# A depthwise convolution shared between VectorE and TensorE: 128 and 64 channels in place of 96 and 96, two taps a product, two products side by side, the image loop written out

## The reference, cut to the phase

```python
D, inner = 96, 192                    # k_conv has shape (3, 3, 1, inner): depthwise
DECAY, GAIN = 0.6, 0.4                # of _ema_scan: y[i] = DECAY * y[i-1] + GAIN * x[i]
h  = _layernorm(x, n1_g, n1_b)
p  = h @ w_in + b_in                  # 96 -> 192 channels
p  = depthwise 3x3 convolution of p with k_conv, zero padding
p  = p + 0.25 * (scans of p along both axes, forward and backward)
p  = _layernorm(p, on_g, on_b)
x  = x + p @ w_out + b_out            # 192 -> 96 channels
```

## Time and profile before

| | us |
|---|---|
| median of 3 runs | 1366.96 |
| lowest, highest | 1360.24, 1372.87 |
| the profiled execution | 1367.83 |
| its span in the profile | 1366.0 |
| TensorE, VectorE busy in the span | 1183.3 (87%), 741.9 (54%) |
| ScalarE, POOL busy | 510.8 (37%), 391.8 (29%) |

### The profile page before, as it was taken

How to read it: one execution, slowest core, us unless ns; L and a number is a source line. 1 busy time by engine, 2 the same in 40 slices (tenths; PEclk the granted TensorE clock), 3 DMA queues, 4 the chain that set the end, 5 groups by cost and what they waited for, 6 DMA issues and landing times. The chain is left out here.

```text
span 1366.0 us, 24417 instructions
## 1 busy us (share of the span) xinstructions
PE 1183.3 (87%) x8951; PEld 812.9 (60%) x8951; DVE 741.9 (54%) x2104; ACT 510.8 (37%) x823; POOL 391.8 (29%) x599
## 2 busy tenths in 40 slices
PE   0599989699996979999999997786988978799998
PEld 0266656477775656666667664564454544477776
DVE  1578873367774426666666666474355565232322
ACT  0266643233331333333343331442443422254553
POOL 1356636433433530110110210313200000344432
PEclk9899999899996999999999998788799999799999
DMA  5320000000000000000000000000000000000000
GB/s 67 67 53 2 2 1 1 0 1 0 0 0 1 0 0 1 1 1 1 1 1 1 1 1 1 1 1 1 1 2 1 2 1 1 1 7 13 6 12 12
DMA packets 27297, 9.16 MB, mean 7 GB/s; under 512 B 25345, under 2 KB 27200, under 8 KB 27200
## 3 DMA queue, kind: packets, MB, share of 16 engines
q1 hardware_dynamic: 24720, 7.13, 2.8%
q10 hardware_dynamic: 2480, 0.73, 0.4%
HBM read 6.27 MB, written 1.57 MB: 6 GB/s over the span
## 5 line engine op out<-in xcount | busy, mean ns | idle before, releaser
L142 POOL TENSOR_TENSOR ln_v<-MV,eps 128x2 f32<-128x2 f32 (+3 forms) x81 | 16.1, 199 | 433.6 <-PE bank L1064 246.0
L1126 ACT ACTIVATE fa_e<-bank 128x1024 f32<-128x1024 f32 x64 | 65.5, 1024 | 159.5 <-PE bank L1034 159.5
L1876 PEld LDWEIGHTS bank<-e_w,ex_G 128*128 128x128 f32 x768 | 90.7, 192 | 14.8 <-issue 14.6
L1981 DVE SCALAR_TENSOR_TENSOR X<-bank,ex_L,X 128x96 f32<-128x96 f32 (+1 forms) x128 | 31.7, 310 | 121.1 <-PE bank L1876 113.0
L1178 DVE TENSOR_REDUCE fa_z<-bank 128x4 f32<-128x1024 f32 x64 | 78.3, 1223 | 25.1 <-PE bank L1016 23.3
L1868 PE MATMUL bank<-hT,e_w 96*128 96x512 f32 x192 | 91.0, 610 | 0.0
L1876 PE MATMUL bank<-e_w,ex_G 128*128 128x96 f32 x768 | 90.0, 274 | 0.0
L1918 ACT ACTIVATE ex_G<-bank,e_b 128x512 f32<-128x512 f32 x96 | 64.7, 687 | 63.3 <-PE bank L1868 61.4
L1735 DVE TENSOR_REDUCE ca_z<-bank 128x2 f32<-128x256 f32 x96 | 48.8, 550 | 69.3 <-PE bank L1492 69.2
L1034 PE MATMUL bank<-fa_a,fa_b 64*128 64x256 f32 x512 | 73.5, 406 | 1.1 <-DVE fa_a L1185 1.1
L145 POOL TENSOR_TENSOR ln_r<-ln_v,minus_half 128x2 f32<-128x2 f32 (+3 forms) x81 | 71.7, 885 | 0.0
(11 more groups left out here) (251 smaller groups left out, 2604.0 us busy)
## 6 DMA issues: line engine op xcount, KB each, us to landing
X<-in_x SPq DMA_DIRECT2D x16, 96.0 KB
out_tokens<-X SPq DMA_DIRECT2D x8, 192.0 KB, 2.1
e_w<-in_L_ffn_w SPq DMA_DIRECT2D x2, 576.0 KB
bias0r<-in_L_conv_rpb_table ACTq DMA_DIRECT2D x16, 24.0 KB
m0w<-in_L_conv_mlp_w SPq DMA_DIRECT2D x2, 144.0 KB
m1w<-in_L_conv_w SPq DMA_DIRECT2D x2, 144.0 KB
f_w<-in_L_ffn_W SPq DMA_DIRECT2D x2, 142.5 KB
mixer<-in_mixer SPq DMA_DIRECT2D x1, 256.0 KB
```

Source lines behind the costliest of these rows:

```text
L1126: act.activation(E[v % 2][:], k.banks[:, b:b + 2, :].rearrange("p i (c q) -> p i c q", c=2), ACT.Exp).then_inc(s["exp"], 1)
L1876: last = pe.matmul(bank[6 + e % 2][:, t * C:(t + 1) * C], G[e % 2][:, j, t * P:(t + 1) * P], k.ew2[:, e, j, :], start=(j == 0), stop=(j == ...
```

## The change

The two halves of the convolution get unequal shares: 128 channels for VectorE, which works on partitions in parallel, and 64 for TensorE. TensorE's 64 channels lie twice on the 128 partitions, the second copy shifted by one column of the image, so that a product with K = 128 takes two taps (x = 0 and 1) at once. Nine products become six: three with two taps and three with one (x = 2), whose upper 64 rows of `diag` are zero. They are 64 columns wide and go in turn to partitions 0 to 63 and 64 to 127 of bank 3, so that two lie side by side in the array. Those two sums are added and transposed at once in `conv_t`, by a product with `stack2`, two 64x64 identity matrices on top of each other. `mix` comes after the first pair, and writes bank 7 in place of bank 4. `back` and `conv_t` each begin with one `keep_warm` into bank 4, ahead of their waits. `widened` becomes three activations. `pipeline` becomes `in_turn`, which writes all 16 images out. POOL calls `norm(0, 0)` first and makes `diag` with three products and a memset. The loads grow from 7 transfers to 18, all in `k.late`.

```diff
+def in_turn(steps, body):
+    for n in range(steps):
+        body(n, n % 2, n == 0, n == steps - 1)
...
-    k.win = weight("w_in", [C, CI], a["L1_conv_w_in"])
-    k.bin = weight("b_in", [C, 2], a["L1_conv_b_in"].rearrange("(j p) -> p j", p=C))
-    k.kconv = sb("k_conv", [C, 2, 9])
-    for j in range(2):
-        loads.append((k.kconv[:, j, :], a["L1_conv_k_conv"].rearrange("a b o (j p) -> j p (a b o)", p=C)[j]))
-    k.ong = weight("on_g", [C, 2], a["L1_conv_on_g"].rearrange("(j p) -> p j", p=C))
-    k.onb = weight("on_b", [C, 2], a["L1_conv_on_b"].rearrange("(j p) -> p j", p=C))
-    k.wout = weight("w_out", [C, 2, C], a["L1_conv_w_out"].rearrange("(j p) c -> p j c", p=C))
+    k.win = sb("w_in", [C, 2 * P])
+    loads.append((k.win[:, 0:CI], a["L1_conv_w_in"]))
+    loads.append((k.win[:, CI:2 * P], a["L1_conv_w_in"][:, P:CI]))
+    k.bin, k.ong, k.onb = sb("b_in", [P, 2]), sb("on_g", [P, 2]), sb("on_b", [P, 2])
+    k.kconv, k.wout = sb("k_conv", [P, 2, 9]), sb("w_out", [P, 2, C])
+    k.stack2 = weight("stack2", [P, CI - P], a["stack2"])
+    for j, p0, channels in ((0, 0, slice(0, P)), (1, 0, slice(P, CI)), (1, CI - P, slice(P, CI))):
+        rows = slice(p0, p0 + channels.stop - channels.start)
+        for t, name in ((k.bin, "b_in"), (k.ong, "on_g"), (k.onb, "on_b")):
+            loads.append((t[rows, j:j + 1], a["L1_conv_" + name][channels, None]))
+        loads.append((k.kconv[rows, j, :], a["L1_conv_k_conv"].rearrange("a b o p -> p (a b o)")[channels]))
+        loads.append((k.wout[rows, j, :], a["L1_conv_w_out"][channels]))
...
+        NARROW = CI - P
+        part = (P, NARROW)
-        acc = [sb(f"acc{i}", [C, TOK]) for i in range(2)]
-        acc1 = sb("accb", [C, TOK])
-        diag = sb("diag", [P, 9, C])
+        acc = [sb(f"acc{i}", [P, TOK]) for i in range(2)]
+        acc1 = sb("accb", [P, TOK])
+        diag = sb("diag", [P, 6, NARROW])
...
             def _(pool):
                 k.clear_retired()
-                pool.memset(diag[:], 0.0)
+                norm(0, 0)
                 for i in range(2):
                     last = pool.memset(grid[i][:], 0.0)
                 last.then_inc(s["init"], 1)
                 pool.wait_ge(s["init"], 1)
-                for tap in range(9):
-                    last = pool.tensor_scalar(diag[0:C, tap, :], k.ident[0:C, 0:C], k.kconv[:, 1, tap:tap + 1], 0.0, ALU.mult, ALU.add)
+                for i in range(2):
+                    pool.tensor_tensor(diag[low, 3 * i:3 * i + 3, :], k.stack2[low, None, :].broadcast_to([NARROW, 3, NARROW]),
+                                       column[low, 2 * i, :, None].broadcast_to([NARROW, 3, NARROW]), ALU.mult).then_inc(s["diag"], 1)
+                pool.tensor_tensor(diag[high, 0:3, :], ...
+                pool.memset(diag[high, 3:6, :], 0.0).then_inc(s["diag"], 1)
...
                 def back(n):
+                    keep_warm(pe, k, bank[4][:])
                     pe.wait_ge(s["z2"], n + 1)
...
-                            last = pe.transpose(bank[5][0:C, (2 * j + t) * P:(2 * j + t + 1) * P], Z[:, t, j * C:(j + 1) * C], k.ident[:])
+                            last = pe.transpose(bank[5][0:part[j], (2 * j + t) * P:(2 * j + t + 1) * P], Z[:, t, j * P:j * P + part[j]], k.ident[:])
...
-                            last = pe.matmul(o, ZT[:, j, t, :], k.wout[:, j, :], start=False, stop=(j == 1))
+                            last = pe.matmul(o, ZT[0:part[j], j, t, :], k.wout[0:part[j], j, :], start=False, stop=(j == 1))
...
-                    for tap in range(9):
-                        if tap == 2 and not first:
+                    for i in range(6):
+                        if i == 2 and not first:
                             mix(n - 1)
-                        y, x = divmod(tap, 3)
-                        last = pe.matmul(bank[3][0:C, 0:TOK], diag[:, tap, :], grid[slot][:, 1, y:y + SIDE, x:x + SIDE],
-                                         start=(tap == 0), stop=(tap == 8))
+                        y, single = i % 3, i // 3
+                        last = pe.matmul(bank[3][64 * (i % 2):64 * (i % 2) + 64, 0:TOK], diag[:, i, :],
+                                         grid[slot][:, 1, y:y + SIDE, 2 * single:2 * single + SIDE],
+                                         start=(i < 2), stop=(i > 3), skip_group_check=True)
...
                 def conv_t(n, slot):
+                    keep_warm(pe, k, bank[4][:])
                     pe.wait_ge(s["conv"], 9 * (n + 1))
...
-                    for half, src in ((0, acc[slot]), (1, acc1)):
-                        for j in range(2):
-                            last = pe.transpose(bank[2][:, (2 * j + half) * C:(2 * j + half + 1) * C], src[:, j * P:(j + 1) * P], k.ident[0:C, 0:C])
+                    for t in range(2):
+                        tok = slice(t * P, (t + 1) * P)
+                        pe.transpose(bank[2][:, t * CI:t * CI + P], acc[slot][:, tok], k.ident[:])
+                        last = pe.matmul(bank[2][:, t * CI + P:(t + 1) * CI], acc1[:, tok], k.stack2[:], start=True, stop=True)
...
-                    for j in range(2):
-                        last = act.activation(grid[slot][0:C, j, 1:1 + SIDE, 1:1 + SIDE],
+                    for rows, j, x in ((slice(0, P), 0, 1), (slice(0, NARROW), 1, 1), (slice(NARROW, P), 1, 0)):
+                        last = act.activation(grid[slot][rows, j, 1:1 + SIDE, x:x + SIDE],
```

More of the change, by code:

```diff
@@ L738, in _ @@
                 pool.wait_ge(s["init"], 1)
-                for tap in range(9):
-                    last = pool.tensor_scalar(diag[0:C, tap, :], k.ident[0:C, 0:C], k.kconv[:, 1, tap:tap + 1], 0.0, ALU.mult, ALU.add)
-                last.then_inc(s["diag"], 1)
+                low, high = slice(0, NARROW), slice(NARROW, P)
+                column = k.kconv[:, 1, :].rearrange("p (y x) -> p x y", x=3)
+                for i in range(2):
+                    pool.tensor_tensor(diag[low, 3 * i:3 * i + 3, :], k.stack2[low, None, :].broadcast_to([NARROW, 3, NARROW]),
+                                       column[low, 2 * i, :, None].broadcast_to([NARROW, 3, NARROW]), ALU.mult).then_inc(s["diag"], 1)
+                pool.tensor_tensor(diag[high, 0:3, :], k.stack2[high, None, :].broadcast_to([NARROW, 3, NARROW]),
+                                   column[high, 1, :, None].broadcast_to([NARROW, 3, NARROW]), ALU.mult).then_inc(s["diag"], 1)
+                pool.memset(diag[high, 3:6, :], 0.0).then_inc(s["diag"], 1)
+                pool.wait_ge(s["diag"], 4)
                 def rstd2(n):
@@ L769, in mix @@
                         for j in range(2):
-                            last = pe.matmul(bank[4][:, t * CI:(t + 1) * CI], k.mixer[:, j, t * P:(t + 1) * P], loc[:, j, :],
+                            last = pe.matmul(bank[7][:, t * CI:(t + 1) * CI], k.mixer[:, j, t * P:(t + 1) * P], loc[:, j, :],
                                              start=(j == 0), stop=(j == 1))
@@ L803, in widen @@
                     for j in range(2):
-                        last = pe.matmul(bank[1][0:C, j * TOK:(j + 1) * TOK], k.win[:, j * C:(j + 1) * C], k.hT[slot][:, 0:TOK], start=True, stop=True)
+                        last = pe.matmul(bank[1][:, j * TOK:(j + 1) * TOK], k.win[:, j * P:(j + 1) * P], k.hT[slot][:, 0:TOK], start=True, stop=True)
                     last.then_inc(s["in"], 1)
@@ L830, in _ @@
                 widen(0, 0)
-                pe.wait_ge(s["diag"], 1)
+                pe.wait_ge(s["diag"], 4)
                 def body(n, slot, first, last):
@@ L856, in zt @@
                     for j in range(2):
-                        last = act.activation(ZT[:, j, :, :], bank[5][0:C, j * 2 * P:(j + 1) * 2 * P].rearrange("p (t q) -> p t q", t=2),
-                                              ACT.Identity, bias=k.onb[:, j:j + 1], scale=k.ong[:, j:j + 1])
+                        n_rows = part[j]
+                        last = act.activation(ZT[0:n_rows, j, :, :], bank[5][0:n_rows, j * 2 * P:(j + 1) * 2 * P].rearrange("p (t q) -> p t q", t=2),
+                                              ACT.Identity, bias=k.onb[0:n_rows, j:j + 1], scale=k.ong[0:n_rows, j:j + 1])
                     last.then_inc(s["zTe"], 1)
@@ L886, in body @@
                     after(act, s["ct"], n)
-                    act.activation(acc1[:], bank[3][0:C, 0:TOK], ACT.Copy).then_inc(s["acc1"], 1)
+                    act.activation(acc1[:], bank[3][:, 0:TOK], ACT.Copy).then_inc(s["acc1"], 1)
                     if not first:
@@ L903, in norm2 @@
                     for t in range(2):
-                        last = dve.bn_stats(st2[:, t, :], bank[4][:, t * CI:(t + 1) * CI])
+                        last = dve.bn_stats(st2[:, t, :], bank[7][:, t * CI:(t + 1) * CI])
                     last.then_inc(s["bn2"], 1)
@@ L915, in norm2b @@
                     for t in range(2):
-                        last = dve.tensor_scalar(Z[:, t, :], bank[4][:, t * CI:(t + 1) * CI], ag2[:, t, 0:1], r2[:, t, :], ALU.subtract, ALU.mult)
```

(1 more changed line is left out.)

22 lines of the change are left out of this document (11 added, 11 removed).

## The result

| | median, us | runs | lowest, highest |
|---|---|---|---|
| before | 1367.4 | 4 | 1360.2, 1372.9 |
| after | 1391.8 | 4 | 1388.5, 1393.6 |

The ratio is 1.018 (95% interval 1.013 to 1.023): the changed kernel is slower by 24 us. The profiled execution of after has a span of 1391.8 against 1366.0.

The account below looks back on a forecast made before the run. A chain over all engines, 9.54 us from one `back` to the next, was taken as the bound. 1367.8 + 4.4 (images) - 4.6 (start) = 1367.6, + 14.3 for the falling clock = 1382 us; range 1360 to 1400.

Parts of the forecast that it names:

- The bound: Convolution mixer: a chain over all engines, 9.54 us from one `back` to the next, bounds it, not TensorE.
- The taps: `taps` on TensorE: falls from 4.0 to about 1.5 us an image, most of it going into the wait for Z.
- The clock: TensorE in the mixer: 2.4 us idle ahead of `back` brings half speed 30% of the time, +14.3 us.
- Shapes of 64: Array shape changes around `out` and `back`: +0.13 us an image, bounds 0 and +0.4.
- keep_warm ahead of `conv_t`: Behind `out`, on the chain: +0.22 us an image; the one in `back` is hidden by idle time.
- `conv_t` and the taps pair: Link from `out` to `mix`: longer `conv_t` +0.34, shorter first pair about -0.36; net taken as +0.05 us an image.
- Third activation: `widened` on ScalarE: +0.41 us, covered by 0.2, so 0 on the chain, upper bound +0.2.
- Start: Start of the stage: POOL's flags first -4.1, first image's shorter TensorE work -0.5; sum -4.6 us, bounds -2 and -7.
- Unrolled, loads: Mixer images written out: -1.6 us over twelve images; eleven more small DMAs in window attention: 0.
- The clock holds: TensorE in the mixer: two keep_warm and dense work between gaps keep full speed, 1368 us; chance 0.27.
- The taps were the bound: TensorE's fullness causes the wait for Z, so the mixer's period falls to say 8.0 us, 1341 us; chance 0.07.
- The clock returns late: TensorE in the mixer stays at half speed longer: half the time low 1393 us, nearly all 1430; chance 0.07.

Follow-up runs that it names:

- the six-tap kernel: The kernel before with six of TensorE's nine taps, three products left out and nothing in their place: 1379.1 us, ratio 1.010.
- the reordered kernel: The changed kernel with `out` on 128 rows, `out(n-2)` in place of `out(n-1)`, `widen` ahead of `back`, more keep_warm ahead of `back`: 1345.2 us, ratio 0.984.
- the one-shape kernel: The changed kernel with the second product of `out` on all 128 rows, the upper 64 of ZT zeros: 1379.6 us, ratio 1.011.
- the one-shape kernels: Changed kernels with `out` on 128 rows; the times cited are from the one with nine keep_warm in `back` too: 1365.5 us, ratio 1.000.
- The old taps with the new order: The kernel before with images written out, POOL's flags first and `diag` by three products on 96 rows: 1361.1 us, ratio 0.996.
- the two kernels of 10.28 us an image: The changed kernel without both keep_warm matmuls (1372.3 us, ratio 1.005), and with the one in `back` alone (1376.0 us, ratio 1.007).

## Why the prediction was right, and where it was off

*The bound.* Right. TensorE at 92% was not the bound: taking a third of its taps away left the period at 9.55 to 9.65 (the six-tap kernel), and filling it up again left it at 10.45. The links sum up to the period before and after the change, and in the reordered kernel, for which the sum was the forecast.

*The taps.* Right: six products take 1.6 us of an image in two groups (0.58 and 1.02), for a forecast of 1.5, the wait for Z was forecast at 2.4 after the keep_warm and is 2.09.

*The clock.* The mechanism was right and the size low. I had 30% of the time at low clock and +14.3 for fourteen images; the mean clock of 0.88 means 24% of the time, and the price was +18.2 in the six long images among them and +2.7 in the last period, where I had nothing. The term that was mis-sized is the cost of a low stretch. I spread it evenly over the image, 14.35 against 9.86, which at 24% gives only some +11; but in the long image read above the low stretch lies on `out`, `conv_t` and the first part of `mix`, where all of TensorE's time is on the chain, and not in the wait for Z, where it costs nothing. So a quarter of the time costs 3.0 us in six of the fourteen images. (The recorded sum has small slips of its own: a quarter gives +11.7 and a half +25.6, not 11.6 and 25.8.)

*What was luck.* I argued that the clock falls from the length of the gap and its coming back. The kernel without keep_warm has a longer gap, 2.41 us for 2.09, and holds its clock for thirteen images. At the period that I forecast, 9.85, the clock does fall (the one-shape kernel, 1379.6 us); at 10.28, only 0.17 us below the 10.45 of the changed kernel, the medians of the two kernels were 1372.3 and 1376.0. Nothing in the forecast could tell these apart.

*Shapes of 64.* This step failed by its size. I took +0.13, with 0.4 as the upper bound, and it is +0.60, outside of it. I had one change of shape in the rows, 0.1 us, and eight changes an image; I discounted that to 0.13 where the plain product is 0.8. The one-shape kernel shows the 0.60 to be that of the alternating rows in `out` alone. The two records with 64 rows, which the rows above show merged with those ahead of them:

```profile
280.06 0.46 PE L807 MATMUL bank<-w_out,cm_zT 64*128 64x96 f32 x2
```

From 280.06 to the next group 0.39 us pass, where two records of this line take 0.22 in the one-shape kernels (331.15 to 331.59 for four). The two with 128 rows ahead of them take 0.32 for 0.22 (279.74 to 280.06), and the permutation behind them 0.30 for 0.23 (280.45 to 280.75, 331.59 to 331.82). So time is lost going into the 64 rows and coming out of them, about 0.15 for each of the four changes. The Trainium skill, "TensorEngine Tiling (Array Packing)", Key Properties, says that a change of tiling mode drains TensorE; the estimate of 0.8 that I worked out from that rule and the 0.1 of the row, and set aside, was closer than 0.13, though the page has no price and the 0.60 comes from four changes and not from eight.

*keep_warm ahead of `conv_t`.* Forecast +0.22; the two kernels with and without it differ by 0.17. Right. That the one in `back` is hidden: right, 10.28 with and without.

*`conv_t` and the taps pair.* +0.05 forecast; the link from `out` to `mix` rose by 0.27, of which 0.17 to 0.23 is keep_warm, so 0.04 to 0.1. `mix` to statistics rose by 0.12, which I hadn't listed; in the earlier trace rows the weights of `mix` were loaded behind taps in the same shape, now behind a pair in another. That this is the cause wasn't tried.

*Third activation.* Right: 1.31 for 0.83, and no link is longer by it.

*Start.* -4.6 forecast, -5.9 measured: -3.9 for the order (-4.1), and -2.0 for the first image, where I had -0.5; the six products at low clock took 2.83 us in place of 5.79, and `widen(1)` came that much earlier. The old taps with the new order gave -2.7 up to the first Z product, so the two terms don't simply add.

*Unrolled, loads.* Right: 1.6 us for thirteen periods in the kernel before. Where the loads are issued SP's queue waits 107.7 us for TensorE in place of the 117.3 of the earlier trace rows.

*Sum.* The stage was forecast at +14.1 and came at +27.2. The signs were all right; the links +12.1 for +4.4, the clock +20.8 for +14.3, and the start 1.3 better make 13 us; the other phases gave back 1.4, and between the medians 1382 was 10 us too low.

*The rivals.* "The clock holds" at 1368: not in the changed kernel; the two kernels of 10.28 us an image held it for thirteen of fifteen periods, with medians of 1372.3 and 1376.0. "The taps were the bound" fell with the six-tap kernel. "The clock returns late" didn't come about: it was back within each long image.

*What stays open.* Why the clock holds for thirteen images at 10.28 us and falls sooner at 9.55 to 9.65 with a gap of 1.70 or 2.41, at 9.85 with 2.09, at 10.38 with 2.51 and at 10.45 with 2.09. The runs rule out the gap's length and the busy share as the only cause, and suggest the period; they don't show how it acts. There is one trace for each kernel, and a second execution of the same kernel may put its falls elsewhere.

## What to carry to other kernels

Before taking work from the busiest engine, sum the chain of one image from start to start: if it closes on the period and the engine waits on it even briefly, the work you take away turns into idle time. On TensorE that isn't free: a gap of some 2 us that comes back each image can bring its clock down, and then less work makes a slower kernel. Shorten the chain first, here by moving `out` away from between Z and `conv_t`, and look for short matmuls in which 64 rows alternate with 128; a product padded with zeros to the shape of its neighbours was 0.27 us faster a group of three.

## What the runs showed that I had not expected

- A tenth of a microsecond an image went with an earlier fall of the clock: at 10.28 us an image with 2.41 us idle not in the first thirteen periods of the profiled execution, at 10.38 with 2.51 in four of them.
- Three matmuls of 96 columns with 128, 128 and 64 rows take 1.01 us (279.44 to 280.45) where the same with 128 rows throughout take 0.74 (330.85 to 331.59) and, with 128, 96 and 96 rows, 0.74 (286.82 to 287.56) before.
- Removing three of nine products from the kernel before cost 14 us.
